# Attention and MoE on one core: a reworked start, a ring of four, and down products held to the end

## The reference

```python
x = L0_attn_x                                    # (2, 1024, 128) float32
# attention: 8 heads, 2 kv groups, head dim 128, latent 32
q = (ln(x) @ wq);  k_lat = ln(x) @ wk_down;  v_lat = ln(x) @ wv_down
k = k_lat @ wk_up; v = v_lat @ wv_up
probs = softmax(causal(q @ k.T * 128**-0.5))
x = x + ln((probs @ v) @ wo)                     # ln: layer norm without scale or shift
# MoE: 32 experts of 64, 16 anchors of 32, one shared expert of 64
h = ln(x)
scores = sigmoid(h @ gate_weight.T)              # groups 2 of 4, then top 6 of 32
routed = sum_e cw[e] * (silu(h @ w_gate[e]) * (h @ w_up[e])) @ w_down[e]
shared = silu(h @ shared_w_gate) * (h @ shared_w_up) @ shared_w_down
anchor = (silu(h @ a_gate[l]) * (h @ a_up[l])) @ a_down[l]   # l from the best expert
x = x + ln(routed + shared + 0.1 * anchor)
```

## Time and profile before

| what | value |
|---|---|
| median of 3 runs | 387.68 us (386.87 to 387.89) |
| the profiled execution's own time | 385.38 us |
| its span | 383.3 us |
| TensorE | busy 367.3 us (96%) |
| GpSimd | busy 283.9 us (74%) |
| VectorE | busy 281.7 us (73%) |
| ScalarE | busy 237.6 us (62%) |
| granted TensorE clock | 0.998 of full speed |

### The profile page before, as it was taken

The page is one execution under the profiler, slowest core; times in us unless marked ns, Lnnn a source line. Parts: engine busy times, 40 slices in busy tenths (PEclk is TensorE's granted clock), DMA queues, the critical chain, the costliest instruction groups (busy, mean ns, idle before and its releaser), DMA issues.

```text
span 383.3 us, 6864 instructions
## 1 busy us (share of the span) xinstructions
PE 367.3 (96%) x2012; PEld 251.7 (66%) x2012; DVE 281.7 (73%) x767; ACT 237.6 (62%) x476; POOL 283.9 (74%) x336
## 2 busy tenths in 40 slices
PE   8989989999999999999999999999999999999992
PEld 8765534654555654445467887778878888788871
DVE  5998997986977887455468865859767687567764
ACT  4658865795655667753964557856575645665652
POOL 6215847399999998997689785899937997396651
PEclk9999999999999999999999999999999999999999
DMA  7159872903205006000000000010000000010000
GB/s 233 33 77 187 145 178 50 196 21 60 26 2 84 3 2 86 1 4 2 2 3 0 1 0 2 0 31 1 0 0 2 27 3 0 0 29 0 0 1 27
DMA packets 12690, 14.55 MB, mean 38 GB/s; under 512 B 1520, under 2 KB 9136, under 8 KB 12656
## 3 DMA queue, kind: packets, MB, share of 16 engines
q1 hardware_dynamic: 12096, 13.36, 18.3%
q10 hardware_dynamic: 560, 0.77, 0.6%
HBM read 6.26 MB, written 1.05 MB: 19 GB/s over the span
## 4 chain that ended last, share of the span: by engine, by line
PE 72%; POOL 8%; ACT 6%; issue 5%; DVE 4%; DMA 2%; SPq 1%; ACTq 0%; POOLq 0%; DVEq 0%
PE ps L1367 10%; PE ps L1368 10%; PE ps L1369 10%; PE ps L1485 6%; PE ps L1467 6%; POOL probs L898 5%; PE ps L1568 5%; PE ps L1498 5%; PE ps L1570 5%; PE ps L1571 5%; PE ps L1508 3%; PE ps L1518 2%; DMA raw<-in_ffn_w_up 2%; ACT probs L1096 2%; ACT normed_p L1037 2%
## 5 line engine op out<-in xcount | busy, mean ns | idle before, releaser
L971 POOL TENSOR_TENSOR silu<-silu,cwb 128x512 f32<-128x512 f32 x80 | 102.5, 1294 | 33.1 <-ACT silu L1124 28.3
L1096 ACT ACTIVATE probs<-ps 128x512 f32<-128x512 f32 (+1 forms) x152 | 78.6, 580 | 37.9 <-PE ps L1485 17.6
L898 POOL TENSOR_TENSOR probs<-probs 128x1024 f32<-128x1024 f32 (+3 forms) x56 | 92.3, 1673 | 8.1 <-PE ps L1498 7.8
L1330 DVE TENSOR_TENSOR ps<-silu,ps 128x512 f32<-128x512 f32 (+1 forms) x84 | 57.8, 693 | 20.8 <-POOL silu L971 18.9
L1124 ACT ACTIVATE silu<-ps 128x512 f32<-128x512 f32 x80 | 47.7, 597 | 36.8 <-PE ps L1369 27.5
L1338 DVE TENSOR_TENSOR h_lo<-ps,h_hi 128x512 fp32r<-128x512 f32 x80 | 54.3, 685 | 21.0 <-ACT h_hi L1136 20.5
L1256 DVE TENSOR_REDUCE nmax_h<-ps 128x1 f32<-128x512 f32 (+3 forms) x96 | 59.7, 674 | 12.3 <-PE ps L1470 6.8
L1136 ACT ACTIVATE h_hi<-ps 128x512 fp32r<-128x512 f32 (+1 forms) x84 | 49.9, 598 | 27.7 <-DVE ps L1330 26.6
L1367 PE MATMUL ps<-xT_hi,w_hi 128*128 128x512 f32 x164 | 65.6, 400 | 0.2 <-ACT silu L1124 0.2
L1368 PE MATMUL ps<-xT_lo,w_hi 128*128 128x512 f32 x164 | 64.3, 392 | 0.0
L1369 PE MATMUL ps<-xT_hi,w_lo 128*128 128x512 f32 x164 | 64.2, 391 | 0.0
(11 more groups left out here) (195 smaller groups left out, 512.4 us busy)
## 6 DMA issues: line engine op xcount, KB each, us to landing
qst<-q_hi SPq DMA_DIRECT2D x14, 256.0 KB, 5.6
qst<-q_lo SPq DMA_DIRECT2D x7, 256.0 KB, 6.9
x_sb<-in_attn_x SPq DMA_DIRECT2D x4, 256.0 KB, 6.1
raw<-in_ffn_w_gate SPq DMA_DIRECT2D x5, 192.0 KB, 7.0
raw<-in_ffn_w_up SPq DMA_DIRECT2D x5, 192.0 KB, 7.3
raw<-in_ffn_w_down SPq DMA_DIRECT2D x5, 192.0 KB, 7.3
kst<-k_hi SPq DMA_DIRECT2D x6, 128.0 KB, 3.3
result<-x_sb SPq DMA_DIRECT2D x3, 256.0 KB, 2.3
```

The costliest lines, as they stand in the source:

```text
L898: nc.gpsimd.tensor_tensor(into, into, probs[:, BUF[n, kt], j:end, cols], ALU.add).then_inc(added, 1)
L971: nc.gpsimd.tensor_tensor(silu[:, k % HRING, :], silu[:, k % HRING, :], cwb[:, m % 2, t // ET, :], ALU.mult).then_inc(scaled_ready, 1)
L1096: nc.scalar.activation(probs[:, BUF[n, kt], j:j + w, at:at + cols], bank(full)[:, 0:w * cols].rearrange("p (w c) -> p w c", w=w), ACT.Exp) ...
L1330: nc.vector.tensor_tensor(up, silu[0:rows, k % HRING, :], up, ALU.mult).then_inc(h_ready, 1)
```

## The change

- Chunk 0 is loaded in four transfers of one tile, each with its semaphore; bn_stats of a tile waits for its own transfer only.
- Its tile 2 is normalised on GpSimd (`xn_nrm0p`), tiles 0 and 1 on VectorE, tile 3 on ScalarE. The transposes of tiles 0 and 1 wait for VectorE only. Tiles 0 and 1 go into one bank, 2 and 3 into the next, and `xT_hi` and `xT_lo` of chunk 0 are made in two halves of 256 columns. `a3_hi` comes after `xT_hi`.
- The planner has a landing for each chunk, and the moments of chunks 1, 2 and 3 come after `xn_nrm0`, `xT_lo` of chunk 0 and the last `q0_lo`, each after the moments before it.
- `masked_by_max` holds only for n > 2, so blocks 1 and 2 are masked by a matmul.
- `HRING` is 4. The last six `down` products (k = 78 to 83) get rank 100 + NU, behind every `g` and `u`.
- `TILE_SHY` is 0.4 and `SEED` is 120.

```diff
-HRING = 3
+HRING = 4
+LATE_DOWNS = 6
...
-    return h == BLOCKS[n][1] and wide == 1 and n > 0
+    return h == BLOCKS[n][1] and wide == 1 and n > 2
...
+MOM_AFTER = {1: (("xn_nrm0",),), 2: (("xT_lo", 0),), 3: (("q0_lo", REP - 1),)}
...
-TILE_IN, TILE_OUT, TILE_STAY, TILE_SHY = 10, 19, 0.3, 0.5
-SEED, WOBBLE = 11, 0.04
+TILE_IN, TILE_OUT, TILE_STAY, TILE_SHY = 10, 19, 0.3, 0.4
+SEED, WOBBLE = 120, 0.04
...
-    step("landing", ("late_in",), 500, 0.3)
+    step("landing", ("late_in",), 150, 0.3)
+    for c in range(1, NCH):
+        step("landing", ("x_in", c), 85, 0.3 + 0.1 * c)
...
-    step("ACT", ("a3_hi",), 45, 1.05, ("am",))
+    step("ACT", ("a3_hi",), 45, 1.05, ("am",), ("xT_hi", 0))
...
-    step("DVE", ("xn_mom", 0), 150, 1, ("x_first",))
+    step("DVE", ("xn_mom", 0), 110, 1, ("x_first",))
...
+    step("POOL", ("xn_nrm0p",), 75, 1, ("xn_rstd", 0))
...
-    step("PE", ("xT", 0), 31, 1, ("xn_nrm", 0), ("xn_nrm0",), bank=1, until=("xT_lo", 0))
+    step("PE", ("xT", 0), 31, 1, ("xn_nrm", 0), ("xn_nrm0",), ("xn_nrm0p",), bank=2, until=("xT_lo", 0))
...
-    step("ACT", ("xT_hi", 0), 60, 1, ("xT", 0))
-    step("DVE", ("xT_lo", 0), 69, 1, ("xT_hi", 0))
+    step("ACT", ("xT_hi", 0), 45, 1, ("xT", 0))
+    step("DVE", ("xT_lo", 0), 45, 1, ("xT_hi", 0))
...
-        step("DVE", ("xn_mom", c), 126, rank, ("late_in",), ("xn_nrm", c - 1), ("xT_lo", 0) if c == 1 else ("q0_lo", REP - 1))
+        step("DVE", ("xn_mom", c), 126, rank, ("x_in", c), ("xn_mom", c - 1), *MOM_AFTER[c])
...
-        step("PE", ("down", k), 68 if t != SHARED else 45, rank - 3, ("lo", k), ...
+        step("PE", ("down", k), 68 if t != SHARED else 45, rank - 3 if k < NU - LATE_DOWNS else 100 + NU, ("lo", k), ...
...
+        def xT0_half(half):
+            return ps[:, BANK["xT", 0] + half, 0:CH // 2]
...
-                    sp.dma_start(rows_of(0), x_rows[:, 0:TPC, :]).then_inc(x_in[0], 16)
+                    for t in range(TPC):
+                        sp.dma_start(x_sb[:, t, :], x_rows[:, t, :]).then_inc(x0_in[t], 16)
...
+                elif kind == "xn_nrm0p":
+                    k = LN["xn_mom", 0]
+                    t = TPC - 2
+                    pool.wait_ge(rstd0_ready, 1)
+                    nc.gpsimd.tensor_scalar(normed_x[:, t, :], x_sb[:, t, :], rstd[:, k, t:t + 1], offset[:, k, t:t + 1], ALU.mult, ALU.add).then_inc(normed0_pool, 1)
...
+                elif ev == ("xT_hi", 0):
+                    act.wait_ge(xT0_begun, 1)
+                    nc.scalar.activation(xT_hi[:, 0:CH // 2], xT0_half(0), ACT.Copy).then_inc(xT0_hi_begun, 1)
+                    act.wait_ge(misc_full, MISC["xT", 0])
+                    nc.scalar.activation(xT_hi[:, CH // 2:CH], xT0_half(1), ACT.Copy).then_inc(hi_ready, 1)
...
-                    for t in range(TPC - 1):
+                    for t in range(TPC - 2):
...
+                elif ev == ("xT_lo", 0):
+                    dve.wait_ge(xT0_hi_begun, 1)
+                    nc.vector.tensor_tensor(xT_lo[:, 0:CH // 2], xT0_half(0), xT_hi[:, 0:CH // 2].bitcast(F32), ALU.subtract)
+                    dve.wait_ge(hi_ready, HI["xT_hi", 0])
+                    nc.vector.tensor_tensor(xT_lo[:, CH // 2:CH], xT0_half(1), xT_hi[:, CH // 2:CH].bitcast(F32), ALU.subtract).then_inc(lo_ready, 1)
...
+                        if ev == ("xT", 0) and t == TPC - 2:
+                            last.then_inc(xT0_begun, 1)
+                            pe.wait_ge(normed0_pool, 1)
+                            pe.wait_ge(normed_ready, NORMED[nrm])
+                        to = xT0_half(t // 2)[:, P * (t % 2):P * (t % 2) + P] if ev == ("xT", 0) else bank(ev)[:, P * t:P * t + P]
+                        last = nc.tensor.transpose(to, normed_of(nrm)[:, t, :], ident[:])
```

More of the change, by code:

```diff
@@ L651, in build @@
         x_in = [sem(f"x_in{c}") for c in range(NCH)]
+        x0_in = [sem(f"x0_in{t}") for t in range(TPC)]
         small_in = sem("small_in")
```

18 lines of the change are left out of this document (12 added, 6 removed).

## The result

| | before | after |
|---|---|---|
| median (7 runs each, same chip) | 387.01 us | 382.94 us (381.57 to 384.79) |
| ratio, 95% interval | | 0.9896 (0.9875 to 0.9918) |
| the profiled execution, its span | 385.38, 383.3 us | 382.94, 381.1 us |
| its granted clock | 0.998 | 0.990 |

The change makes the kernel 4.1 us faster. The forecast was 1.6 us, with a range that ended at 383.9: the sign was right, the size was not.

The account below looks back on a forecast made before the run. It took TensorE as the bound from 200 us on and no single engine before. Front -0.2, moments -0.4, masks +0.4 and tail -1.4 summed to -1.6 us, the median going from 387.68 to 386.1, range 383.9 to 388.9.

Parts of the forecast that it names:

- The new order: Planner's picks throughout under new seed and TILE_SHY: priced by 0.2 us per visit to column-tiled products, taken as 0.
- rival 3: Order comes out better and early chunks fill the gaps: another 1.5 to 2 us, 384.4; chance 0.17.
- The ring of four: Deeper buffers from 200 us on, where TensorE is full: 0 to 0.3 us lost, taken as 0.
- The tail: End of the kernel: held-back down products follow the last u, 1.4 us gained, bounds 1.0 to 1.5.
- The masks: Blocks 1 and 2, 25 to 55 us: 16 more mask matmuls on TensorE, taken as 0.4 us lost.
- the nearer bound: Masks of blocks 1 and 2 hidden behind VectorE: -0.5 us, against +1.9 if paid in full.
- The front: Start of the kernel, chunk 0: 0.2 us gained, bounds 0.5 gained to 0.6 lost.
- the four transfers: Chunk 0's load in four: moments start no earlier since VectorE was late; 0 gained, perhaps 0.3 us lost.
- The halves: xT_hi and xT_lo of chunk 0 in two halves: last xT_lo ends at 10.3, 0.5 us sooner.
- rival 4: Chunk 1 lands late and holds xT_lo back: 387.0, chance 0.05; its sign is k0 starting after 11.
- GpSimd beside VectorE: Normalising chunk 0 on both: they shut each other out, done about 8.5 under am; without that cover worth 0.3 us.
- The early moments: Moments moved forward let later chunks' turns and projections fill gaps: 0.4 us gained, bounds 0 to 1.2.

Follow-up runs that it names:

- b_ring4: The kernel before with HRING = 4 alone, its own seed: 386.33 us, ratio 0.9997, lowest 385.91.
- a_ring3: The changed kernel with HRING = 3, planned anew: 384.92 us, ratio 0.9962, lowest 383.46.
- a_masks_back: The changed kernel in the same order, with blocks 1 and 2 masked on VectorE again: 382.45 us, ratio 0.9897, lowest 381.36.
- b_s66: The kernel before with SEED 66 and TILE_SHY 0.4, its best of 160 seeds by planned end: 386.08 us, ratio 0.9976, lowest 384.36.
- b_masks_s47: The kernel before with blocks 1 and 2 masked by matmul, planned anew with SEED 47, TILE_SHY 0.4: 384.30 us, ratio 0.9957, lowest 383.80.
- a_nomask_s35: The changed kernel with blocks 1 and 2 masked on VectorE, planned anew with SEED 35, TILE_SHY 0.5: 384.46 us, ratio 0.9927, lowest 381.48.
- a_one_load: The changed kernel in the same order, with chunk 0 in one transfer: 381.90 us, ratio 0.9907, lowest 381.40.
- a_one_hold3: The changed kernel in the same order, chunk 0 in one transfer and the fill cut from 12 matmuls to 6 (HOLD 3): 381.78 us, ratio 0.9892.
- b_mt_s47: The kernel before with matmul masks of blocks 1 and 2, ring of four and late downs, planned anew with SEED 47: 383.26 us, ratio 0.9921, lowest 382.11.
- b_mtm_s56: The kernel before with matmul masks, ring of four, late downs, and the changed landings and moments, SEED 56: 382.88 us, ratio 0.9913, lowest 382.59.
- a_same: The changed kernel itself, run again on another round's chip, against the kernel before: 381.79 us, ratio 0.9881, lowest 381.49.

## Why the prediction was wrong

**The new order: the step that failed.** "The new order ... I take 0", with 1.6 us to either side, priced by one thing that a row showed, the visits; and the visits hardly changed (38 to 40). What an order is worth is the waiting that it leaves between matmuls, of which I had named three gaps and which is 5.2 us less in the changed kernel, a good half of it ahead of the last shift. Other seeds lose 3.7 and 4.0 us between lowest runs, as much as the whole change, so no term of the sum could be right while the order was left out. Under rival 3 I wrote "Against: the seed was only exchanged for another". As far as it goes that is so: seed 11 was as good for the old lists as 120 is for the new ones. What the sum left out is what the edits let the planner do. Its own ends, 382.78 and 378.20 us, could have been had before any run, and 4.6 us sooner is close to what was measured; I had worked it through for the first steps only. Rival 3 (0.17, 384.4) had the mechanism, and its price was 1.5 us short.

**The ring of four: taken at 0, measured at 2.** "From 200 us TensorE is full already, so deeper buffers give nothing there." TensorE's busy share is the wrong witness, as the prediction itself had said of an earlier stretch: a matmul shown for 0.39 us hides up to 0.16 us of waiting. With the kernel's old order the step holds (b_ring4); with the changed one it does not (a_ring3). About 0.75 us of it is the tail, where the ring of three holds `h_hi` back, as the prediction said it would ("The ring of four is what allows it"); it had only charged the ring with none of that. Why the other 1.2 us appear in the MoE part of one order and not of the other stays open.

**The tail: right in its mechanism, 0.9 in place of 1.4.** The three held products do follow the last `u` without a gap and product 82 waits for `h_lo`. The forecast had one wait of 0.2 us; there are two, of 0.45 and 0.38. The bound had named the engine: `h` and `h_lo` at 0.69 us each on VectorE against 1.38 us of products. For product 81, `h_lo` starts 0.19 us late, behind `h_hi` of ScalarE. For 82 the sum had forgotten a step: `h` of product 83 stands on VectorE ahead of `h_lo` of 82 (371.25 and 371.84), although `h_hi` of 82 was out at 371.10:

```profile
369.76 0.70 DVE L1362 TENSOR_TENSOR ps<-silu,ps 128x512 f32<-128x512 f32 x1
370.01 1.09 ACT L1160 ACTIVATE h_hi<-ps 128x512 fp32r<-128x512 f32 x2
370.64 0.69 DVE L1370 TENSOR_TENSOR h_lo<-ps,h_hi 128x512 fp32r<-128x512 f32 x1 [0.19 <-ACT h_hi L1160]
371.25 0.68 DVE L1362 TENSOR_TENSOR ps<-silu,ps 64x512 f32<-64x512 f32 x1
371.84 0.68 DVE L1370 TENSOR_TENSOR h_lo<-ps,h_hi 128x512 fp32r<-128x512 f32 x1
```

**The masks: +0.4 forecast, about 0 measured.** In a held order they cost nothing that can be seen (a_masks_back), so most of the 1.9 us on TensorE is hidden, as the nearer bound said. The 16 matmuls are there:

```profile
L1508 PE MATMUL ps<-mask_row,ident_bf x48: 230/258/650, 16.3 to 165.3; 128*128 128x128 bf16 x24, 128*128 128x256 bf16 x16, 128*128 128x512 bf16 x8
```

What they do for the order, planned anew, is not settled: between b_s66 and b_masks_s47 it is 0.6 us by the lowest runs and 0.2%, or 0.7 us, by the ratios, between a_nomask_s35 and the changed kernel nothing by the lowest runs and 0.3% or more by the ratios.

**The front: -0.2 forecast, +0.2 to +1.1 measured at shift 0, for two reasons.** First, "0 gained, perhaps 0.3 lost" for the four transfers, "because VectorE was the one that was late". With four transfers VectorE is not late: the small weights are there 0.6 to 0.9 us earlier, and the moments begin 0.8 us earlier or more. But the tiles landed 0.6 to 0.9 us apart in after, so the last moment came 0.75 later and `am` was no cover any more. The price varies between executions, and its average of some 0.15 us lies inside the forecast; the reason given for it was wrong. The Trainium skill (DMA: Bandwidth & Descriptors, "Rules for kernel authors") says that many small transfers are better joined, being mostly overhead under 64 KB. The four transfers here are of 64 KB, at the edge of that; the trace agrees in that the last quarter is used later than the whole was, and the times of a_one_load show no difference. Second, `am2`. The diff changes the modelled landing of the late inputs from 500 to 150, and the planner then puts `am2` ahead of `k0` and behind the fill. The prediction does not name it, though the line was in the diff. Fill and `am2` together hold `k0` 0.9 us beyond `xT_lo`, and of that a_one_hold3 takes back 0.7. The halves did what was forecast: `xT_lo` ends 1.64 us after the first transpose in place of 2.03, 0.4 us sooner where 0.5 was said, and `am2` ate it. The moments of chunk 1 ran before `xT_lo`, which followed them at once and ended as soon as was hoped after the first transpose, so `k0` after 11, my sign of rival 4, had another cause.

**GpSimd beside VectorE.** Of the two normalisations on VectorE one took 653 ns, with the one of GpSimd (512 ns) beside it:

```profile
L1240 DVE TENSOR_SCALAR normed_x<-x_sb,rstd,offset x2: 345/499/653, 8.3 to 8.6; 128x128 f32<-128x128 f32 x2
...
L863 POOL TENSOR_SCALAR normed_x<-x_sb,rstd,offset x1: 512/512/512, 8.4 to 8.4; 128x128 f32<-128x128 f32 x1
```

The two VectorE tiles take 0.92 us, as three did: the third engine took a tile away and gave no time back. The Trainium skill's rule (SBUF — State Buffer, "Who interferes with whom"), that the two shut each other out for a whole instruction, agrees with that; the 0.3 us that the prediction would have given the part without the cover of `am` was not there.

**The early moments: -0.4 forecast, not shown.** Between b_mt_s47 and b_mtm_s56 the medians say 0.4 us faster and the lowest runs 0.5 slower.

**The sum.** Between the traces of a_same and before, TensorE's last matmul comes 2.9 us sooner: front +1.1, order and masks -1.6 between the shifts, the late downs -0.9, and another -1.5 behind shift 7, which goes when the ring goes. The forecast had -0.2, 0, 0 and -1.4. The lowest runs differ by more (385.5 and 381.5, 4.0 us), because the profiled execution of before was one of its fastest and that of a_same had the latest first shift of its kind.

## What to carry to other kernels

Where a planner with a seed makes the lists, an edit can't be judged at one seed: hold the order to price the edit alone, and choose the best seed for each version before comparing versions. Where the planner runs without the chip, run it for both versions before forecasting: its end is an estimate of the very term that is hardest to work out from rows. A constant of the planner's model, here a landing time, is part of a change like any instruction: follow it to the first step that it moves. And splitting a transfer for an engine that waits is no gain by itself: VectorE was waiting here, it began 0.8 us earlier or more, and the last quarter still made it end up to 0.9 us later.
